# Two-layer graph network on one core: left scores through memory, a reordered front, a third adjacency pair held on chip, degrees from layer 1, and the last pair by tile

## The chip, the core and the metric

The kernel runs on one core of a Trainium2 chip. The engines of the core work side by side, each through its own list of instructions in order: TensorE (PE, with its weight loads PEld), VectorE (DVE), ScalarE (ACT), GpSimd (POOL), and SyncE (SP), which here only issues transfers. They wait for each other on semaphores. The metric is the device time of one execution, in microseconds (us); smaller is better.

## What is computed

```
deg = max(sum(adj != 0), 1)
h   = relu(layernorm(x))                                   # x: 3327 x 256, adj: 3327 x 3327, zeros and ones
x   = x + L0(h, adj)
h   = relu(layernorm(x))
x   = x + relu((dinv * (adj + I) * dinv @ h + h) @ W + b)  # dinv = rsqrt(deg)

L0(x, adj):
  attn_a = sigmoid([adj @ x, x] @ Wa.T + ba);  attn_b the same with Wb, bb
  h = x @ W_sa;  s_left = h @ a_sa[:256];  s_right = h @ a_sa[256:]
  e = where(adj != 0, exp(-leaky_relu(s_left[:, None] + s_right[None, :], 0.01)), 0)
  x_a = (e / (sum(e, axis=1) + 1e-5)) @ h
  x_b = adj @ (x @ W_gcnb) + b_gcnb
  return sigmoid(attn_a * x_a + attn_b * x_b)
```

The "layer 1" of the title is the first of the two layers (the one with scores), "layer 2" below the last one. In the code names with a trailing 1 (`dense1`, `HI1`, `pooled`) belong to the last layer.

## The kernel before

The 3327 rows stand in 26 tiles of 128, taken as 13 pairs (`PAIRS`); `LAST` is 12. Wide products are made of 16-bit halves, `HI` and `LO` of a value, so that each product of two matrices is two or three matmuls per tile.

**The front** (first loop on PE, `for s in range(PAIRS)`) prepares `h` of pair after pair. Per pair `s`: ACT normalises (`norm`, line 448), PE turns the tile (`turn`, L610), ACT copies it twice (`turned`, L455 and L456), DVE makes the low half (`turned_second`, L899), PE projects to six score columns (`project`, L638), DVE takes them (`take_scores`, L907), PE multiplies with both weights (`dense`, 12 matmuls of 512 columns, L656 to L658), ACT and DVE take the two halves `HI` and `LO` (`first_halves` L469, `second_halves` L914). DVE also takes the statistics of two later pairs (`row_stats`, L843, L847), POOL their inverse deviations (`inv_stds`, L327, L329). The left score of every row has to stand in every partition: POOL spreads it on a diagonal (`diag`, L337), PE multiplies that with ones (`widen`, L644), and ACT copies it (`left`, L473) to `slw`, which shares its memory with `LO1`. `keep_busy` (L622) gives PE matmuls on ones whose result nobody reads: 42 ahead of the first `dense`, and 4 behind each of the first two. From step 4 on PE does the first products of layer 1 in between (`neighbours` with m = 0 on the adjacency, `unit` on the exponentials).

**Layer 1** goes over the pairs `m`: ACT makes the exponentials of pair m (`leaky` L485, `expo` L494), DVE masks and splits them (L939, L945), PE does 13 `unit`s (12 matmuls each, L703 to L705) and 13 `neighbours` (8 matmuls each, L682 and L683) of the pair behind. The adjacency of a pair is loaded by POOL's queue to `stage`, transposed by DVE (`turn_adj`, L931) to one of two buffers `adjT`, and stored by SP's queue to memory (`adjT_store`).

**Layer 2** (`pooled(k, u)`, L754 and L755, 8 matmuls) takes the pairs in the order `ORDER` = 11, 12, 0, 1, ..., 10. The first two are still in the two `adjT` buffers; each later one is loaded back in two chunks (u below 6, and the rest) by SP as soon as the buffer's last chunk is done (L292). Three accumulators take turns. A column of ones behind `HI1` gives the degrees; DVE's `output` (L1100 to L1117) takes the maximum with 1, the inverse, adds the self term from POOL and the residual, and ACT's queue stores 256 KB per pair.

What sets the order everywhere is the order in which each engine's list is written; an engine that waits holds all that stands behind.

Of the kernel before, what the change touches and what calls it, by code (L numbers as in the profile page):

```python
# [19 lines left out]
def gnn_kernel(nc, x, adj, W_sa, a_sa, W_g, b_g, Wa, ba, Wb, bb, W1, b1, out):  # L20
# [29 lines left out]
    with ExitStack() as ctx:  # L50
# [8 lines left out]

        adjT_store = nc.dram_tensor("adjT_store", [PAIRS, P, PAIRS * 256], U32, kind="Internal").ap()  # L60
# [4 lines left out]
        HI1 = sb("HI1", [P, TILES, D + 2], F16)  # L65
# [25 lines left out]
        diag = sb("diag", [P, 2, P])  # L91
# [11 lines left out]
        degm = sb("degm", [P, 2])  # L103
        drp = sb("drp", [P, 2])
        drw = sb("drw", [P, 2])
# [24 lines left out]
        slw = LO1[:].rearrange("p (m e) d -> p m (e d)", e=2).bitcast(F32)  # L130

# [42 lines left out]
        diag_ok = sem("diag_ok")  # L174
        wide = sem("wide")
        sl_ok = sem("sl_ok")
# [42 lines left out]
        one1_ok = sem("one1_ok")  # L219
        lo1_ok = sem("lo1_ok")  # L220
        adj_ld = [[sem(f"adj_ld{c}_{b}") for b in range(2)] for c in range(NC)]
# [6 lines left out]
        deg_c = sem("deg_c")  # L228
        drp_ok = sem("drp_ok")
        drw_ok = sem("drw_ok")  # L230
        pt_c = sem("pt_c")
# [28 lines left out]
        def out_count(k, b):  # L260
            return 16 * sum(3 if ORDER[j] == LAST else 1 for j in range(k + 1) if j % 2 == b)
# [4 lines left out]
        def _(sp):  # L266
            for k, w in enumerate((W_sa, W_g)):
                sp.dma_start(wsg[k], w.rearrange("(h p) o -> p h o", p=P)).then_inc(wsg_in, 16)
            load_x(sp, 0, (2, 3))
# [7 lines left out]
            sp.dma_start(w1, W1.rearrange("(h p) o -> p h o", p=P)).then_inc(w1_in, 16)  # L277
            sp.dma_start(bgrep[:], bass.AP(b_g.tensor, 0, [[0, P], [1, D]])).then_inc(rep_in, 16)
            sp.dma_start(b1rep[:], bass.AP(b1.tensor, 0, [[0, P], [1, D]])).then_inc(rep_in, 16)

            for m in range(LAST - 1):
                sp.wait_ge(tr_ok, NC * (m + 1))
                sp.dma_start(adjT_store[m], adjT[m % 2][:].rearrange("p u e i v -> p (u e i v)").bitcast(U32)
                             ).then_inc(stored[m % 2], 16)
            for b in range(2):
                sp.wait_ge(stored[b], 16 * len(range(b, LAST - 1, 2)))

            for k in range(2, PAIRS):
                for c, (u0, u1) in enumerate(CHUNKS):
                    sp.wait_ge(part_done[c], k - 1)  # L290
                    dst = adjT[(k + 1) % 2][:, u0:u1].rearrange("p u e i v -> p (u e i v)").bitcast(U32)
                    sp.dma_start(dst, adjT_store[ORDER[k], :, 256 * u0:256 * u1]).then_inc(adj_ld[c][k % 2], 16)  # L292
# [853 lines left out]
```

## Time and profile before

| | us |
|---|---|
| median of 3 runs | 653.65 |
| lowest, highest | 652.34, 656.84 |
| profiled execution, device time | 648.95 |
| its span, first to last instruction | 647.1 |
| PE busy in it | 617.8 (95%) |
| DVE, ACT, POOL busy | 438.2, 365.3, 271.5 |

The profile shows one execution. PE's matmuls overlap, so that a busy PE may still start matmuls at a slow pace; how many it starts in a stretch and the clock it was granted say more. Idle time ahead of an instruction is listed with what ended it. Idle time of an engine that nobody waits for costs nothing.

### The profile page before, as it was taken

The numbers are of one execution on the slowest core, as the hardware profiler recorded it, in microseconds if no ns is written. First come the engines' busy times: TensorE is split into PE (matmuls) and PEld (weight loads), VectorE is DVE, ScalarE is ACT, GpSimd is POOL, SyncE is SP. The second block draws the span as 40 slices with busy tenths as digits, with TensorE's granted clock in tenths as the row PEclk, the third lists the DMA queues.
The fourth block names the chain that finished last, engine by engine and source line by source line (L and its number), as shares of the span: only waits on it lengthen the run. The fifth ranks groups of instructions, "written<-read, shape, count | busy, mean of one in ns | idle before, by whom it ended". The sixth has DMA issues, their size and how long they took to land.

```text
span 647.1 us, 13487 instructions
## 1 busy us (share of the span) xinstructions
PE 617.8 (95%) x5333; PEld 528.0 (82%) x5333; DVE 438.2 (68%) x869; ACT 365.3 (56%) x877; POOL 271.5 (42%) x378
## 2 busy tenths in 40 slices
PE   6777999999999999999999999999999799999994
PEld 3445677888888888888888888888888688888883
DVE  4577665799999898989898988988752323122131
ACT  2566676779888787878787777879632000000000
POOL 3547463355435162435353366313134253425331
PEclk9798999999999999999999999999999999999998
DMA  8904572397364554656563644000010365555521
GB/s 201 194 4 131 81 170 44 50 195 180 51 164 89 124 142 74 156 80 160 73 164 53 164 50 58 2 1 2 1 51 2 115 244 172 171 161 178 183 76 32
DMA packets 38549, 68.62 MB, mean 106 GB/s; under 512 B 3159, under 2 KB 30809, under 8 KB 37079
## 3 DMA queue, kind: packets, MB, share of 16 engines
q0 software_dynamic: 28544, 22.15, 23.6%
q1 hardware_dynamic: 7906, 41.68, 19.8%
q10 hardware_dynamic: 2037, 3.94, 2.3%
q8 instruction: 42, 0.69, 0.4%
q14 instruction: 20, 0.16, 0.1%
HBM read 67.74 MB, written 22.15 MB: 139 GB/s over the span
## 4 chain that ended last, share of the span: by engine, by line
PE 87%; POOL 4%; DVE 3%; issue 2%; DMA 1%; ACT 1%; ACTq 0%; POOLq 0%; DVEq 0%
PE accE L703 11%; PE accE L705 11%; PE accA L682 11%; PE accE L704 11%; PE accA L683 11%; PE accA L755 8%; PE accA L754 8%; PE accE L754 4%; PE accE L755 4%; POOL diag L337 1%; PE tp L610 1%; POOL stage L317 1%; PE pw L726 1%; PE pw L727 1%; PE pw L728 1%
## 5 line engine op out<-in xcount | busy, mean ns | idle before, releaser
L703 PE MATMUL accE<-HI,Z 128*128 128x257 f16 x676 | 184.3, 273 | 0.0
L705 PE MATMUL accE<-HI,E 128*128 128x257 f16 x676 | 184.1, 272 | 0.0
L704 PE MATMUL accE<-LO,Z 128*128 128x256 f16 x676 | 183.9, 272 | 0.0
L485 ACT ACTIVATE Z<-LO,sr 128x256 f32<-128x256 f32 x338 | 151.3, 497 | 40.0 <-PE accE L705 40.0
L682 PE MATMUL accA<-HI,adjT 128*128 128x258 f16 x676 | 154.1, 273 | 0.0
L683 PE MATMUL accA<-LO,adjT 128*128 128x258 f16 x676 | 154.0, 273 | 0.0
L494 ACT ACTIVATE Z<-Z,sr 128x256 f32<-128x256 f32 x338 | 150.2, 497 | 0.1
L945 DVE TENSOR_TENSOR E<-Z 128x512 bf16<-128x512 f32 x169 | 140.7, 832 | 5.8
L939 DVE TENSOR_TENSOR Z<-adjT,Z 128x512 f32<-128x512 bf16 x169 | 120.3, 712 | 18.8 <-ACT Z L494 18.6
L755 PE MATMUL accA<-LO,adjT 128*128 128x256 f16 x468 | 103.5, 273 | 0.0
L754 PE MATMUL accA<-HI,adjT 128*128 128x257 f16 x468 | 103.5, 273 | 0.0
L317 POOL DMA_DIRECT2D stage<-in_adj_dram x96 | 59.6, 655 | 98.8 <-DVE adjT L931 94.5
L683 PEld LDWEIGHTS accA<-LO,adjT 128*128 128x128 bf16 x676 | 66.0, 98 | 8.9
L682 PEld LDWEIGHTS accA<-HI,adjT 128*128 128x128 bf16 x676 | 66.0, 98 | 8.8
L704 PEld LDWEIGHTS accE<-LO,Z 128*128 128x128 bf16 x676 | 65.8, 97 | 8.4
L705 PEld LDWEIGHTS accE<-HI,E 128*128 128x128 bf16 x676 | 65.7, 97 | 8.5
L703 PEld LDWEIGHTS accE<-HI,Z 128*128 128x128 bf16 x676 | 65.8, 97 | 8.4
L423 POOL TENSOR_TENSOR late<-HI,LO 128x512 f32<-128x512 f16 x13 | 20.0, 1538 | 79.8 <-DVE wx L1112 77.8
L931 DVE STREAM_TRANSPOSE adjT<-stage 128x768 uint32<-128x768 uint32 (+1 forms) x52 | 51.0, 1017 | 0.0
L754 PE MATMUL accE<-HI,adjT 128*128 128x257 f16 x208 | 47.2, 278 | 3.9 <-DMA adjT<-adjT_store 3.9
L754 PEld LDWEIGHTS accA<-HI,adjT 128*128 128x128 bf16 x468 | 45.8, 98 | 5.7
L755 PEld LDWEIGHTS accA<-LO,adjT 128*128 128x128 bf16 x468 | 45.8, 98 | 5.3
(116 smaller groups left out, 761.6 us busy)
## 6 DMA issues: line engine op xcount, KB each, us to landing
adjT_store<-adjT SPq DMA_DIRECT2D x11, 1664.0 KB, 6.7
adjT<-adjT_store SPq DMA_DIRECT2D x11, 896.0 KB, 4.7
stage<-in_adj_dram POOLq DMA_DIRECT2D x48, 192.0 KB, 5.0
adjT<-adjT_store SPq DMA_DIRECT2D x11, 768.0 KB, 6.3
stage<-in_adj_dram POOLq DMA_DIRECT2D x36, 224.0 KB, 8.1
out_dram<-late ACTq DMA_DIRECT2D x12, 256.0 KB
stage<-in_adj_dram POOLq DMA_DIRECT2D x12, 223.5 KB, 9.7
xs<-in_x_dram SPq DMA_DIRECT2D x5, 256.0 KB, 6.0
```

What stands on the lines that cost most here:

```text
L317: pool.dma_start(stage[32 * b:32 * b + 32, :, :, w0:w1_], src).then_inc(adj_in[c], 16)
L485: ins = act.activation(Z[:, n % RING, v], slw[:, m], ACT.Relu, bias=sr99[:, t:t + 1], scale=1.0 - SLOPE)
L494: ins = act.activation(Z[:, n % RING, v], Z[:, n % RING, v], ACT.Exp, bias=sr01[:, t:t + 1], scale=-1.0)
L682: pe.matmul(dst, w, HI[:, t, G0:HIW], start=(t == 0), stop=False)
L683: ins = pe.matmul(dst, w, LO[:, t, D:LOW], start=False, stop=(t == TILES - 1))
L703: pe.matmul(dst[:, 0:D + 1], zhi, HI[:, t, 0:D + 1], start=(t == 0), stop=False)
L704: pe.matmul(dst[:, 0:D], zhi, LO[:, t, 0:D], start=False, stop=False)
L705: ins = pe.matmul(dst[:, 0:D + 1], zlo, HI[:, t, 0:D + 1], start=False, stop=(t == TILES - 1))
L754: pe.matmul(dst[:, 0:D + 1], w, HI1[:, t, 0:D + 1], start=(t == 0), stop=False)
L755: ins = pe.matmul(dst[:, 0:D], w, LO1[:, t, :], start=False, stop=(t == TILES - 1))
L939: dve.tensor_tensor(Z[:, n % RING], rows, Z[:, n % RING], ALU.mult).then_inc(mask_ok, 1)
L945: dve.tensor_tensor(E2[:, n % RING], Z[:, n % RING], hi, ALU.subtract).then_inc(e2_ok, 1)
```

## The change

1. **Left scores through memory.** `diag`, `widen` and `left` are gone. SP stores the column of left scores of a pair (128 x 2 numbers of 4 bytes) to `sl_store` in memory, waits until it is there, and loads it back to all partitions (128 KB) as `slw`. `project` now waits for `srw_ok` where it waited for `left`.
2. **Front reordered.** SP loads half of the first x group ahead of `W_sa`; ACT's queue loads the other half, then `W_g`. DVE takes the first statistics before the weights' scales. The first `dense` stands ahead of `turn(1)` and `project(0)`; ACT's `norm(1)` stands behind `first_weights`. `W1` and the two bias rows are loaded behind the first left scores.
3. **No idle products.** `keep_busy` is gone.
4. **Third pair kept.** In layer 2 the memory of `stage`, free by then, is a third adjacency buffer. The pair k = 2 is loaded to it during layer 1, and each pair k from 3 on goes where k - 3 was. PE's order at the change of layers takes `pooled(2, u)` where it took the last `pooled(0, u)` and `pooled(1, u)`.
5. **Degrees from layer 1.** The ones column comes in with `neighbours`: its first matmul has 260 columns instead of 258, the second still 258, written two columns further on. ACT copies the degree column per pair; DVE forms the inverse once for all tiles. `pooled` has 256 columns instead of 257 in its first matmul, and `output` is three instructions on DVE. POOL scales the self term per tile.
6. **Last pair by tile.** The last pair of layer 2 does all its e = 0 matmuls, then all e = 1, with output and store by tile.

```diff
@@ sync
-            for k, w in enumerate((W_sa, W_g)):
-                sp.dma_start(wsg[k], w.rearrange("(h p) o -> p h o", p=P)).then_inc(wsg_in, 16)
-            load_x(sp, 0, (2, 3))
+            load_x(sp, 0, (0, 1))
+            sp.dma_start(wsg[0], W_sa.rearrange("(h p) o -> p h o", p=P)).then_inc(wsg_in, 16)
...
+            def spread_left(i):
+                sp.wait_ge(srw_ok, i + 1)
+                sp.dma_start(bass.AP(sl_store.tensor, 2 * P * i, [[1, P], [P, 2]]), srw[:, 2 * i:2 * i + 2, 3],
+                             allow_slow_non_contiguous=True).then_inc(sl_out, 16)
+                sp.wait_ge(sl_out, 16 * (i + 1))
+                if i >= 1:
+                    sp.wait_ge(sl_in, 16 * i)
+                sp.dma_start(slw[:, i], bass.AP(sl_store.tensor, 2 * P * i, [[0, P], [1, 2 * P]])).then_inc(sl_in, 16)
...
+            for i in range(PAIRS):
+                spread_left(i)
+                if i == 0:
+                    sp.dma_start(w1, W1.rearrange("(h p) o -> p h o", p=P)).then_inc(w1_in, 16)
...
+                if i == 6:
+                    keep_adj(0)
+            for m in range(1, LAST - 1):
+                keep_adj(m)
...
+            sp.wait_ge(tr_ok, NC * PAIRS)
             for k in range(2, PAIRS):
                 for c, (u0, u1) in enumerate(CHUNKS):
-                    sp.wait_ge(part_done[c], k - 1)
-                    dst = adjT[(k + 1) % 2][:, u0:u1].rearrange("p u e i v -> p (u e i v)").bitcast(U32)
+                    if k >= 3:
+                        sp.wait_ge(part_done[c], k - 2)
+                    dst = adj1[k % 3][:, u0:u1].rearrange("p u e i v -> p (u e i v)").bitcast(U32)
...
@@ gpsimd, score_parts
-                if i >= 1:
-                    pool.wait_ge(wide, i)
-                for e in range(2):
-                    ins = pool.tensor_scalar(diag[:, e], ident[:], srw[:, 2 * i + e, 3:4], None, ALU.mult)
-                ins.then_inc(diag_ok, 1)
...
@@ scalar
-            load_x(act, 0, (0, 1))
+            load_x(act, 0, (2, 3))
+            act.dma_start(wsg[1], W_g.rearrange("(h p) o -> p h o", p=P)).then_inc(wsg_in, 16)
...
             def leaky(m, u):
                 n = m * PAIRS + u
-                if n == 0:
-                    act.wait_ge(sl_ok, 1)
+                if u == 0:
+                    act.wait_ge(sl_in, 16 * (m + 1))
...
+                act.activation(degs[:, 2 * m:2 * m + 2], accA[m % 2][:].rearrange("p (e n) -> p e n", e=2)[:, :, 0],
+                               ACT.Copy)
...
@@ tensor, neighbours
-                        dst = bank(accA[m % 2], e)[:, 0:D + 2]
-                        pe.matmul(dst, w, HI[:, t, G0:HIW], start=(t == 0), stop=False)
-                        ins = pe.matmul(dst, w, LO[:, t, D:LOW], start=False, stop=(t == TILES - 1))
+                        dst = bank(accA[m % 2], e)
+                        pe.matmul(dst[:, 0:D + 4], w, HI[:, t, ONE:HIW], start=(t == 0), stop=False)
+                        ins = pe.matmul(dst[:, 2:D + 4], w, LO[:, t, D:LOW], start=False, stop=(t == TILES - 1))
...
@@ tensor, change of layers
-            pooled(0, LAST - 2)
-            pooled(1, LAST - 2)
+            for u in range(2):
+                pooled(2, u)
             turn1(LAST)
-            pooled(0, LAST - 1)
-            pooled(1, LAST - 1)
+            for u in range(2, 5):
+                pooled(2, u)
             dense1(LAST)
-            for u in range(6):
+            for u in range(5, 8):
                 pooled(2, u)
-            pooled(0, LAST)
-            pooled(1, LAST)
-            for u in range(6, PAIRS):
+            for k in range(2):
+                for u in range(10, PAIRS):
+                    pooled(k, u)
+            for u in range(8, PAIRS):
                 pooled(2, u)
-            for k in range(3, PAIRS):
+            for k in range(3, LAST):
                 for u in range(PAIRS):
                     pooled(k, u)
+            for e in range(2):
+                pooled_tile(LAST, e)
...
@@ vector
+            def pooled_out(k, e):
+                t = 2 * ORDER[k] + e
+                dve.scalar_tensor_tensor(out=[wx, wm][k % 2][:, e], in0=bank([accA[1], accA[0], accE][k % 3], e)[:, 0:D],
+                                         scalar=drw[:, t:t + 1], in1=hpw[:, e], op0=ALU.mult,
+                                         op1=ALU.add).then_inc(y_ok, 1)
```

On PE, in the front, these rows stand before from the last matmul of the first `dense` to the first of the second (`accA<-wh` is `dense`, `accA<-ones` is `keep_busy`, `pw<-diag` is `widen`, `tp` is `turn`, `pw<-w` is `project`):

```order
L658 MATMUL accA<-wh,hTl 128x512
L622 MATMUL accA<-ones 128x256 x4
L644 MATMUL pw<-diag,ones 128x256
L610 MATMUL tp<-ident,hf 128x128 x4
L638 MATMUL pw<-w,hT 128x6 x4
L656 MATMUL accA<-wh,hTh 128x512
```

And the same place in the changed kernel:

```order
L667 MATMUL accA<-wh,hTl 128x512
L629 MATMUL tp<-ident,hf 128x128 x4
L652 MATMUL pw<-w,hT 128x6 x4
L629 MATMUL tp<-ident,hf 128x128 x4
L652 MATMUL pw<-w,hT 128x6 x4
L665 MATMUL accA<-wh,hTh 128x512
```

The filling and the `widen` are gone, and `turn(1)` and `project(0)`, which stood ahead of the first `dense`, stand behind it.

On DVE, at the start of the program, before (`wabs`, `ub`, `wmax`, `winv` are the scales of the weights, `bst`, `mv` the statistics of x, `nmr` is what ACT's `norm` waits for, `wl` what `dense` waits for):

```order
L1014 COPY w<-pw 128x4
L1015 COPY w<-pw 128x4
L869 TENSOR_REDUCE wabs<-late 128x1 x2
L869 TENSOR_REDUCE wabs<-w 128x1
L873 TENSOR_SCALAR ub<-ident,wabs 128x128 x3
L843 BN_STATS bst<-xs 128x6 x2
L847 BN_AGGR mv<-bst 128x2 x2
L878 TENSOR_REDUCE wmax<-accE 128x3
L882 TENSOR_SCALAR wmax<-wmax 128x3
L884 RECIPROCAL winv<-wmax 128x3
L853 SCALAR_TENSOR_TENSOR nmr<-mv,rstd 128x2
```

and in the changed kernel:

```order
L862 BN_STATS bst<-xs 128x6 x2
L866 BN_AGGR mv<-bst 128x2 x2
L1035 COPY w<-pw 128x4
L1036 COPY w<-pw 128x4
L888 TENSOR_REDUCE wabs<-late 128x1 x2
L872 SCALAR_TENSOR_TENSOR nmr<-mv,rstd 128x2
L888 TENSOR_REDUCE wabs<-w 128x1
L894 TENSOR_SCALAR ub<-ident,wabs 128x128 x3
```

The first statistics and `nmr` moved ahead of most of the scales; `score_weights` moved behind the weights' low halves.

On SP, at the change of layers, before (with what each waits for):

```order
L283 DMA adjT_store<-adjT 128x3328 [waits tr_ok] x11
L292 DMA adjT<-adjT_store 128x1536 [waits part_done0,stored1,stored0]
L292 DMA adjT<-adjT_store 128x1792 [waits part_done1]
L292 DMA adjT<-adjT_store 128x1536 [waits part_done0]
L292 DMA adjT<-adjT_store 128x1792 [waits part_done1]
```

and in the changed kernel:

```order
L293 DMA adjT_store<-adjT 128x3328 [waits tr_ok] x10
L315 DMA stage<-adjT_store 128x1536 [waits tr_ok,stored1,stored0]
L315 DMA stage<-adjT_store 128x1792
L315 DMA adjT<-adjT_store 128x1536 [waits part_done0]
L315 DMA adjT<-adjT_store 128x1792 [waits part_done1]
```

The first load of layer 2 waits for no matmul of layer 2 any more, and goes to `stage`.

## Rows read from the trace of the kernel before

**Rows 1.** The page, busy time and the granted clock in 40 slices.

```profile
PE 617.8 (95%) x5333; PEld 528.0 (82%) x5333; DVE 438.2 (68%) x869; ACT 365.3 (56%) x877; POOL 271.5 (42%) x378
PEclk9798999999999999999999999999999999999998
```

**Rows 2.** Waits of PE: who waited for whom, total us, times, longest.

```profile
PE pw L644 <- POOL diag L337: 7.1, 6, 2.3
PE accE L754 <- DMA adjT<-adjT_store: 3.9, 1, 3.9
```

**Rows 3.** Stretches: length, busy us (instructions) per engine, clock, DMA share, GB/s.

```profile
19.00:20.00 1.00, 0.71 (x2) 0.29 (x3) 0.96 (x5) 0.00 (x0) 0.00 (x0) 0.50 1.10 217
20.00:30.00 10.00, 8.70 (x38) 4.30 (x37) 5.27 (x22) 4.62 (x9) 6.82 (x13) 0.78 1.25 213
120.00:160.00 40.00, 40.00 (x367) 35.43 (x365) 37.11 (x65) 35.01 (x88) 20.27 (x26) 1.00 0.77 162
510.00:520.00 10.00, 6.14 (x44) 4.70 (x43) 5.62 (x16) 0.00 (x0) 4.84 (x4) 0.83 0.72 279
```

**Rows 4.** Timeline, start of the program: start us, us, instruction, idle before.

```profile
6.64 0.27 PE L627 MATMUL pw<-ident,wrows 8*128 8x8 f32 x1 [1.40 <-DMA wrows<-in_L_gnn_Wb_dram]
12.05 1.09 ACT L448 ACTIVATE hf<-xs,nmr,rstd 128x256 f32<-128x256 f32 x2 [7.50 <-DVE nmr L853]
17.12 1.42 DVE L893 SCALAR_TENSOR_TENSOR wl<-late,winv,wh 128x512 f16<-128x512 f32 x2 [2.80 <-ACT wh L462]
19.29 0.59 PE L656 MATMUL accA<-wh,hTh 128*128 128x512 f16 x1 [0.88 <-DVE hTl L899]
```

**Rows 5.** Timeline, step 2 to step 3 of the front.

```profile
37.35 1.20 POOL L337 TENSOR_SCALAR diag<-ident,srw 128x128 f32<-128x128 f32 x2
38.60 0.70 PE L644 MATMUL pw<-diag,ones 128*128 128x256 f32 x2 [1.59 <-POOL diag L337]
40.75 0.38 PE L656 MATMUL accA<-wh,hTh 128*128 128x512 f16 x1
43.12 0.38 PE L658 MATMUL accA<-wh,hTl 128*128 128x512 f16 x1
```

**Rows 6.** Timeline, first matmul of the `dense` of steps 7 and 12.

```profile
70.56 0.38 PE L656 MATMUL accA<-wh,hTh 128*128 128x512 f16 x1
103.31 0.38 PE L656 MATMUL accA<-wh,hTh 128*128 128x512 f16 x1
```

**Rows 7.** Groups, 19 to 60 us (POOL 0 to 60): count, busy us, mean ns, idle.

```profile
L843 DVE BATCH_NORM_STATS2 bst<-xs 128x6 f32<-128x256 f32 x22 | 8.0, 408 | 0.0
L914 DVE TENSOR_TENSOR LO<-accA,HI 128x512 f16<-128x512 f32 x11 | 7.1, 685 | 6.9 <-ACT HI L469 6.9
L899 DVE TENSOR_TENSOR hTl<-hT,hTh 128x512 f16<-128x512 f32 x7 | 4.8, 685 | 0.0
L931 DVE STREAM_TRANSPOSE adjT<-stage 128x896 uint32<-128x896 uint32 x2 | 2.1, 1082 | 0.0
L329 POOL TENSOR_TENSOR rstd<-ve,halfs 128x4 f32<-128x4 f32 x3 | 3.1, 1038 | 0.2
```

**Rows 8.** Groups of PE over the whole span.

```profile
L644 PE MATMUL pw<-diag,ones 128*128 128x256 f32 x26 | 9.0, 429 | 7.1 <-POOL diag L337 7.1
L682 PE MATMUL accA<-HI,adjT 128*128 128x258 f16 x676 | 154.1, 273 | 0.0
```

**Rows 9.** Transfers: name, queue, count, KB each, median us from issue to landing.

```profile
bias<-in_L_gnn_ba_dram SPq DMA_DIRECT2D x1, 0.5 KB, 5.1
late<-in_L_gnn_W_dram SPq DMA_DIRECT2D x1, 256.0 KB, 16.6
adjT<-adjT_store SPq DMA_DIRECT2D x11, 896.0 KB, 4.7
```

**Rows 10.** Timeline, end of the program.

```profile
638.08 0.22 DVE L1100 TENSOR_SCALAR degm<-accA 128x1 f32<-128x1 f32 x2 [8.60 <-PE accA L755]
639.27 0.88 DVE L1112 SCALAR_TENSOR_TENSOR wx<-wm,drw,late 128x256 f32<-128x256 f32 x2
640.19 0.69 DVE L1117 SCALAR_TENSOR_TENSOR late<-wx,xs 128x512 f32<-128x512 f32 x1
```

More of the change, by code:

```diff
@@ L130, in gnn_kernel @@
         slw = LO1[:].rearrange("p (m e) d -> p m (e d)", e=2).bitcast(F32)
+        adj1 = [adjT[1][:], adjT[0][:],
+                stage[:].rearrange("p e b q -> p (e b q)").rearrange("p (u e i v) -> p u e i v", u=PAIRS, e=2, v=2)]
         accE = ps("accE", 2)
@@ L218, in gnn_kernel @@
         hi1_ok = sem("hi1_ok")
-        one1_ok = sem("one1_ok")
         lo1_ok = sem("lo1_ok")
-        adj_ld = [[sem(f"adj_ld{c}_{b}") for b in range(2)] for c in range(NC)]
+        adj_ld = [[sem(f"adj_ld{c}_{b}") for b in range(3)] for c in range(NC)]
         part_done = [sem(f"part_done{c}") for c in range(NC)]
@@ L260, in out_count @@
         def out_count(k, b):
-            return 16 * sum(3 if ORDER[j] == LAST else 1 for j in range(k + 1) if j % 2 == b)
+            return 16 * sum({LAST: 3, LAST - 2: 2}.get(ORDER[j], 1) for j in range(k + 1) if j % 2 == b)
         block = ctx.enter_context(nc.Block())
@@ L276, in _, with keep_adj @@
             load_x(sp, 3)
[L277 to L281, printed above, removed]
+            def spread_left(i):
[6 more added lines that the diff above has]
+                sp.dma_start(slw[:, i], bass.AP(sl_store.tensor, 2 * P * i, [[0, P], [1, 2 * P]])).then_inc(sl_in, 16)
+            def keep_adj(m):
                 sp.wait_ge(tr_ok, NC * (m + 1))
@@ L414, in _ @@
             inv_std1(LAST)
-            one_column(LAST)
             def self_term(k):
@@ L538, in _ @@
             first_weights(1)
+            norm(1)
             for s in range(PAIRS + 5):
@@ L587, in store_out @@
                 m = ORDER[k]
+                if k == LAST:
+                    for e in range(2):
+                        act.wait_ge(o_ok, k + 1 + e)
+                        dst = bass.AP(out.tensor, (m * 64 + e) * D, [[QN * D, 4], [2 * D, QUAD], [1, D]])
+                        act.dma_start(dst, osb[k % 2][:, e]).then_inc(o_out[k % 2], 16)
+                    return
                 act.wait_ge(o_ok, k + 1)
@@ L618, in turn @@
                 transposes(tp, hf[:, i % 2]).then_inc(hT_ps, 1)
-            def keep_busy(n):
-                for _ in range(n):
-                    pe.matmul(accA[0][:, 0:2 * P], ones[:].bitcast(BF16)[:, 0:P], ones[:].bitcast(BF16), start=True,
-                              stop=True)
             def turn_weights():
@@ L640, in project @@
                 ins.then_inc(proj, 1)
-            def widen(i):
-                pe.wait_ge(diag_ok, i + 1)
-                pe.matmul(pw[:, 256:512], ones[:], diag[:].rearrange("p e n -> p (e n)"), start=True,
-                          stop=True).then_inc(wide, 1)
             def dense(i):
```

167 lines of the change are left out of this document (92 added, 75 removed).

## The prediction

> **What bounds the kernel now.** I read the page first: PE is busy for 95% of the span, the clock row is at 9 or below in a few slices at the front, and 9 elsewhere [rows 1]. A busy PE is not yet a PE that does work at pace, so I went to the stretches. In layer 1 it starts 367 matmuls in 40 us, 0.109 us each, without a gap, at the 2.4 GHz level [rows 3]; there nothing but fewer or shorter matmuls helps. Two stretches are not like that. Between 20 and 30 us PE starts 38 matmuls at a mean clock of 0.78, and between 510 and 520 us it starts 44 where the pace gives 93 [rows 3]. The list of waits then names what PE waited for: 7.1 us for POOL's `diag` in the front, and once 3.9 us for the adjacency that comes back from memory at the change of layers [rows 2]. Last comes the end of the program, where PE has stopped and a chain on DVE and a store remain [rows 10]. So the kernel is PE's list plus a front that several engines share, one hole at the change of layers, and a tail. The change touches all three, and layer 1 hardly.
>
> **The start.** Before, the first `dense` begins at 19.29 [rows 4], behind `norm(0)` at 12.05 on ACT, `norm(1)`, two turns and `project(0)`. Its 12 matmuls of 512 columns run at the 1.2 GHz level (the clock of 0.50 in the first row of [rows 3]), 0.43 us each, 5.1 us. The changed order: x is first in both queues, so I put the first statistics at 5.3 to 6.3, the deviations at 7.4, and `nmr` behind the two large scales at 8.9 (these wait for `wrows`, which PE had at 6.64 [rows 4]; one more transfer ahead of it makes that about 7.0). `norm(0)` 8.9 to 10.1, but `turn(0)` waits in PE's list for the spread of the scales, to 12.0. Two copies to 13.1, two `first_weights` to 14.4, two low halves on DVE (1.42 for both [rows 4]) to 15.2. The first `dense` starts at 15.2, 4.1 us earlier. The 42 idle products ahead of it are worth nothing to it before: it ran at the low level in spite of them [rows 3]. Behind it now stand `turn(1)` and `project(0)`, 1.7 us, `turn(2)`, which waits for `norm(2)` until 23.7, and `project(1)`: the second `dense` begins at 25.2.
>
> **The steps 1 to 6.** From one `dense` to the next PE cannot go faster than dense 2.6 us (12 x 0.216, which is 43.12 - 40.75 over 11 [rows 5]), the high half of one tile on ACT 0.6, and its low half on DVE 0.69 [rows 7]: about 4.1 us. Before, PE's list held `widen` in that path: in step 2 `diag` began on POOL at 37.35, `widen` at 38.60, and the next `dense` at 40.75 [rows 5]. With `diag`, `widen` and `left` gone, what is late next is DVE: two statistics (2 x 2 x 0.41 and the aggregates, 2.0 together), hTl 0.69, LO 2 x 0.69 per step [rows 7], and in steps 1 and 2 it also waits for POOL's deviations, 1.04 [rows 7] behind the statistics. Writing each instruction behind the later of its engine's last one and its releaser, I get `dense` of step 1 to 6 at 25.2, 30.3, 35.7, 39.9, 47.1 and 54.8. Steps 4 and 5 are long since DVE has `turn_adj` (2.1 for its two halves of the second chunk [rows 7]), the scale of `W1` and the first mask there. `dense` of step 7 follows at 60.9, where it was at 70.56 [rows 6].
>
> **The steps 7 to 12.** PE is the bound. From 70.56 to 103.31 are five steps, 6.55 each [rows 6]. A `widen` is two matmuls, 0.43 us [rows 8], and some 0.1 per step was wait for `diag`; 6.03 stay. Step 12 is at 91.0, 12.3 us earlier, and its own `widen` adds 0.4: **12.7 us** if the clock holds at 2.4 GHz.
>
> **The clock.** Fewer matmuls in the gaps let it fall more easily. Before, it was down from before 19 to beyond 24 us although filled, and up afterwards [rows 3]. I charge one of the sparse places (behind the first `dense`, or step 4) two thirds of a `dense` at half pace, 2.6 x 0.65 = **1.7 us**. Front: 12.7 - 1.7 = **11.0 us**. Bounds: 0 to five denses at half pace, 13 us.
>
> **Through memory.** SP's queue carries a store of 256 numbers of 4 bytes and a load of 128 KB per pair. No row has this store; the nearest is the bias, 128 numbers of 4 bytes to 128 partitions, 5.1 us in a busy queue [rows 9]; the worst in that queue is W1's 16.6 [rows 9]. The first left scores are there at 22.4; with the x loads still ahead in the queue I take 6 for the store and 4 for the load, there by 33 (bounds 4 and 33 us for both, from those rows). ACT needs them for the first `leaky` at 39.6: hidden, with 7 us in hand. Behind the waiting SP stand the load of W1, which DVE needs at 42.5 in step 3, and the store of the first adjacency, which DVE needs only after the front. The other 12 pairs are needed one per 30 us in layer 1. Cost 0; each microsecond beyond 39.6 (or for W1 beyond 42.5) would be one on DVE's and PE's path. The Trainium skill (DMA: Bandwidth & Descriptors, "Rules for kernel authors") says that a last dimension which isn't contiguous becomes one descriptor per element, and advises to rearrange it; that rule speaks against this store. By it the cost is in the queue, off the path above, and the sum stays; the rows before can't show its size.
>
> **Layer 1.** 676 matmuls get two more columns [rows 8], 2 / 2.4 ns each, +0.56 us; 676 in layer 2 lose one, -0.28. Together **+0.3 us**. ACT gets one small copy per pair, at most 0.4 us in 30, in a stretch where it is busy 35 of 40 us and PE never waits [rows 3]: 0. Uncovered it would be 13 x 0.4 = 5 us.
>
> **The change of layers.** 93 - 44 = 49 matmuls are missing between 510 and 520 us [rows 3], x 0.109 = **5.4 us**: the wait of 3.9 and the matmuls at half clock behind it. `stage` is free after the last transposition, long before; its load waits for no product of layer 2. Next in line is pair k = 3: its second chunk can be loaded when `pooled(0, 12)` is done, and until it is needed PE has 3 + 5 + 6 groups of 8 matmuls, 12 us, against 4.7 for 896 KB [rows 9]. POOL's self term (about 5 us) and DVE's `output(0)` end inside that time too. All 5.4 are gained.
>
> **The tail.** Before, 638.08 to 640.88 is DVE's chain on 256 rows [rows 10], then the store until 647.1. Now the last tile needs one of the two L1112, 0.44, and half of L1117, about 0.4, with a gap: 0.9 instead of 2.8, **1.9 us**. The store of half the size I count as equal.
>
> **Sum.** 11.0 + 5.4 + 1.9 - 0.3 = 18.0 us. The profiled execution goes from 648.95 to 631. It was 4.7 us under the median of the runs; I take the difference from the median: 653.65 - 18 = **635.5 us**.
>
> **The rivals.**
> *The clock stays low through the front.* For it: without filling the gaps behind each `dense` hold only turns and projections, and around 53 us, before, a light step was already enough to show in the page's row [rows 1]. Against it: between step 2 and 3, before, `dense` found only a `widen`, a turn and a projection ahead of it and still ran at 0.216 per matmul [rows 5]. Price: steps 1 to 5 each some 1.8 us longer, 9 us instead of 1.7; gain 10.7, 643 us. The Trainium skill (TensorE: Matmul & The Clock Gate, "Why this matters for your kernels") asks for TensorE to be kept busy and warns of gaps between bursts; by it this rival is the likelier, and the time is the 643 just worked out. The row of step 2 to 3 says otherwise here, but it had `widen` in it. Chance 0.17.
> *The left scores or W1 come late.* ACT or DVE stands in step 3. With both transfers at the far bound, 33 us from 22.4, that is 55 instead of 39.6, but leaky only holds `unit`: PE loses perhaps 6 us. 641.5 us. Chance 0.09.
> *A new wait takes the place of the load's.* The last turn and `dense1` of the change now find fewer groups ahead, or the self term is late for `output(0)`; the 5.4 stay. 641 us. Chance 0.06.
> *The shifted output slows `neighbours`.* Two matmuls per pair of tiles now write overlapping but unequal columns, the second from the third column on. No row has such a write. It would touch 2 x 676 matmuls; from 18.0 / 1352 = 13 ns more for each the whole gain is gone, and at 25 ns the kernel takes 635.5 + 34 = 669 us, slower. Against it: the forms of 258 and 257 columns with different starts all run at 0.109 us each among each other [rows 3]. Chance 0.03.
>
> **How the numbers follow.** Forecast 0.65; the clock 0.17; late transfers 0.09; new wait 0.06; slower 0.03. The forecast's own range is 631.5 to 639 (the clock term 0 to 4, the start plus or minus 1.5, and the spread of the runs). The range that leaves out no more than 2 in 10 reaches to the clock's 643: 631.5 to 643.5. A measurement of this kernel tells about 1% from no change, 6.5 us: all cases but the last give more in their middle; from the far ends of the clock and the late transfers I leave 0.05 within 1%. Faster 0.92, same 0.05, slower 0.03.
>
> **What would show it.** The first `dense` at about 15, the one of step 7 at about 61, of step 12 at about 91; no `diag` among PE's waits, and in its place, in steps 3 to 5, waits for DVE. No wait for `adjT_store`, and 92 or 93 matmuls in every 10 us around the change of layers. Some 7 us from DVE's first instruction behind the last matmul to the end of the span, instead of 9.0. The load of `sl_store` landed before ACT's first L485. I am wrong if PE waits for ACT or DVE behind a late transfer, if more than one more `dense` runs at 0.43 per matmul, or if layer 1 starts fewer than 365 matmuls in 40 us.

## Result and the profile after

| | before | after |
|---|---|---|
| median (4 runs each, same chip) | 655.25 us | 690.25 us |
| lowest, highest | 652.34, 656.96 | 688.05, 691.98 |
| profiled execution, its span | 648.95, 647.1 | 688.05, 686.2 |
| PE busy in it | 617.8 | 604.7 |

The ratio is 1.0537, interval 1.048 to 1.0594: 5.4% slower, where 2.8% faster was forecast. PE has less to do, 13 us less, and stands still. The page, beside [rows 1]; the two rows are 40 slices of the span (busy share and granted clock in tenths):

```profile
PE 604.7 (88%) x5257; PEld 518.7 (76%) x5257; DVE 424.9 (62%) x809; ACT 361.8 (53%) x877; POOL 259.8 (38%) x352
PE   2889899160099999999999999999999999999997
PEclk9899999685589999999999999999999999999999
PE 73%; DMA 23%; SPq 1%; DVE 1%; issue 0%; ACTq 0%; ACT 0%; DVEq 0%
```

PE stands still twice, from about 120 to 135 us and from 149 to 190 us, and DMA has 23% of the chain that ended last. The list of waits (engine, line, what it waited for: us in total, times, longest), beside [rows 2]:

```profile
DVE adjT L952 <- DMA adjT_store<-adjT: 58.8, 2, 42.9
PE accE L712 <- DVE E L966: 44.2, 5, 40.9
PE accE L712 <- DVE wm L1004: 15.4, 1, 15.4
```

The 7.1 us for `diag` and the 3.9 us for `adjT_store` on PE [rows 2] are gone. In their place DVE waits twice, 58.8 us, for a store: the adjacency of an old pair has to be in memory before DVE may turn a new one into its buffer. PE's two long waits are for DVE behind that. SP's timeline says why the store is late (start us, duration, engine, line, operation; "..." marks more pairs of the same kind):

```profile
21.25 0.40 SPq L284 DMA_DIRECT2D sl_store<-srw  x1
33.74 0.35 SPq L289 DMA_DIRECT2D LO<-sl_store  x1
...
94.80 0.67 SPq L284 DMA_DIRECT2D sl_store<-srw  x1
107.09 0.32 SPq L289 DMA_DIRECT2D LO<-sl_store  x1
107.46 2.06 SPq L293 DMA_DIRECT2D adjT_store<-adjT  x1
...
178.07 0.32 SPq L289 DMA_DIRECT2D LO<-sl_store  x1
178.43 21.32 SPq L293 DMA_DIRECT2D adjT_store<-adjT  x3
```

Each pair's left scores are stored (L284) and waited for; then the load (L289) is issued and SP goes on to the next pair's store, beside which the load lands. Seven pairs take 107.46 - 21.25 = 86 us, 12.3 each. The adjacency of pair 0 is issued behind the seventh, at 107.46, that of pair 1 behind the thirteenth, at 178.43. Before, the first was issued at 56.97. The end of the second hole on the chain that ended last (start, us, what):

```profile
167.71 10.34 DMA sl_store<-srw
...
178.43 8.38 DMA adjT_store<-adjT
...
187.84 0.94 DVE adjT L952
...
190.13 0.40 PE accE L712
```

Three stretches (us, then busy time and starts of PE, weight loads, DVE, ACT, POOL; clock; DMA share; GB/s), two in the second hole and one in layer 1 behind it:

```profile
150.00:160.00 10.00, 0.00 (x0) 0.00 (x0) 0.00 (x0) 0.00 (x0) 0.00 (x0) 0.60 0.20 29
170.00:180.00 10.00, 0.00 (x0) 0.00 (x0) 0.00 (x0) 0.00 (x0) 0.00 (x0) 0.50 0.28 13
200.00:300.00 100.00, 100.00 (x912) 88.67 (x910) 93.16 (x163) 82.03 (x205) 42.52 (x51) 1.00 0.61 130
```

In the hole no engine computes anything, and the transfers move 13 to 29 GB/s: the chip waits for the completion of one transfer of 1 KB at a time. Afterwards layer 1 runs at its old pace, 0.110 us per matmul as in [rows 3].

The difference of the spans, split at places that both traces have: `dense` of step 12 starts at 92.91 instead of 103.31 [rows 6], -10.4. The last transposition in layer 1 starts at 551.39 instead of 502.00, +49.4, so the stretch from step 12 to it gained +59.8. From there to DVE's first instruction behind the last matmul it is 130.2 instead of 136.1, -5.9. From that to the end 4.6 instead of 9.0 [rows 10], -4.4. Together +39.1, which is 686.2 - 647.1. The front's 10.4 us are no gain in the end: the hole ends when SP's chain does, and whoever comes to it earlier waits longer.

### The profile page after: what moved, and what is told of

The parts are those of the page before. It is cut to its first block, busy times and chain, and to the rows that moved or that the text cites. A ratio compares the mean times of both kernels' runs of the same rounds, so it can differ in the third digit from the quotient of the medians.

```text
span 686.2 us, 13267 instructions
## 1 busy us (share of the span) xinstructions
PE 604.7 (88%) x5257; PEld 518.7 (76%) x5257; DVE 424.9 (62%) x809; ACT 361.8 (53%) x877; POOL 259.8 (38%) x352
## 2 busy tenths in 40 slices
DMA packets 44090, 70.33 MB, mean 102 GB/s; under 512 B 6908, under 2 KB 36478, under 8 KB 42620
## 4 chain that ended last, share of the span: by engine, by line
PE 73%; DMA 23%; SPq 1%; DVE 1%; issue 0%; ACTq 0%; ACT 0%; DVEq 0%
DMA sl_store<-srw 22%; PE accE L712 10%; PE accE L714 10%; PE accE L713 9%; PE accA L691 9%; PE accA L692 9%; PE accA L762 7%; PE accA L761 7%; PE accE L762 3%; PE accE L761 3%; DMA adjT_store<-adjT 1%; PE tp L629 1%; PE accA L778 1%; PE pw L736 1%; PE pw L734 1%; PE pw L735 1%
## 5 line engine op out<-in xcount | busy, mean ns | idle before, releaser
L691 PE MATMUL accA<-HI,adjT 128*128 128x260 f16 x676 | 154.2, 274 | 1.3 <-DVE adjT L952 1.3
L960 DVE TENSOR_TENSOR Z<-adjT,Z 128x512 f32<-128x512 bf16 x169 | 120.3, 712 | 18.9 <-ACT Z L507 18.7
L762 PE MATMUL accA<-LO,adjT 128*128 128x256 f16 x416 | 91.6, 273 | 0.0
L761 PE MATMUL accA<-HI,adjT 128*128 128x256 f16 x416 | 91.6, 273 | 0.0
L952 DVE STREAM_TRANSPOSE adjT<-stage 128x768 uint32<-128x768 uint32 (+1 forms) x52 | 51.0, 1018 | 64.1 <-DMA adjT_store<-adjT 58.8
L691 PEld LDWEIGHTS accA<-HI,adjT 128*128 128x128 bf16 x676 | 65.8, 97 | 10.8 <-DVE adjT L952 1.4
L692 PEld LDWEIGHTS accA<-LO,adjT 128*128 128x128 bf16 x676 | 65.9, 97 | 8.8
L762 PE MATMUL accE<-LO,stage 128*128 128x256 f16 x208 | 45.8, 273 | 0.0
L761 PE MATMUL accE<-HI,stage 128*128 128x256 f16 x208 | 45.8, 273 | 0.0
L761 PEld LDWEIGHTS accA<-HI,adjT 128*128 128x128 bf16 x416 | 40.6, 98 | 4.8
L762 PEld LDWEIGHTS accA<-LO,adjT 128*128 128x128 bf16 x416 | 40.7, 98 | 4.7
```

The source lines that it names most:

```text
L691: pe.matmul(dst[:, 0:D + 4], w, HI[:, t, ONE:HIW], start=(t == 0), stop=False)
L692: ins = pe.matmul(dst[:, 2:D + 4], w, LO[:, t, D:LOW], start=False, stop=(t == TILES - 1))
L761: pe.matmul(dst, w, HI1[:, t, :], start=(t == 0), stop=False)
L762: ins = pe.matmul(dst, w, LO1[:, t, :], start=False, stop=(t == TILES - 1))
L960: dve.tensor_tensor(Z[:, n % RING], rows, Z[:, n % RING], ALU.mult).then_inc(mask_ok, 1)
```

## The experiments

The theory after the result (A): SP's list is too slow for what stands behind it, and only the two late adjacency stores cost. Its rival (B): the many small pieces themselves load the DMA engines, whatever the order. And the gains that the prediction counted (front, change of layers, tail) are to be found behind the loss, or not. Kernels with a ratio were run four times; the others once.

**Only SP's order.** Two lines; adjacency stores stand between the left scores:

```diff
-                if i == 6:
-                    keep_adj(0)
-            for m in range(1, LAST - 1):
+                if i in {2: 0, 4: 1, 7: 2, 9: 3}:
+                    keep_adj({2: 0, 4: 1, 7: 2, 9: 3}[i])
+            for m in range(4, LAST - 1):
```

> The changed kernel with SP's list reordered and nothing else: the stores of the adjacency of pairs 0, 1, 2 and 3 stand behind the left scores of pairs 2, 4, 7 and 9 instead of behind those of pair 6 (pair 0) and 12 (the rest). In the changed kernel the profile shows a store of left scores to take 9 to 13 us, thirteen in series on SP, so the adjacency store of pair 0 is issued at 107 us and that of pair 1 at 178 us, and DVE waits 15.9 and 42.9 us for them. Theory A (SP's order: the adjacency stores stand behind a chain of slow round trips): both waits go, 59 us less than the changed kernel, span about 628, ratio to the kernel before about 0.970. Theory B (3328 small descriptors load the 16 DMA engines and slow every transfer): they are all still there, so most of the loss stays, span over 670. Theory C (a wait for the left scores themselves takes over, since they are spread one every 12 us): leaky of a later pair waits; span between 635 and 670.

Measured: 636.78 us, ratio 0.9749 (0.9687 to 0.981), span 633.4. 53 us of the changed kernel's 690 come from the place of four stores. The span is 5 us above the expected 628. No wait for `adjT_store` is left. Its own waits:

```profile
DVE adjT L952 <- DMA stage<-in_adj_dram: 11.8, 3, 8.0
PE accE L712 <- DVE E L966: 7.0, 3, 5.8
```

So something of (B) remains: DVE now waits for POOL's loads of the adjacency. The page's transfers issued from 52 to 90 us (number, KB each, median us to landing), in this kernel and in the one before:

```profile
stage<-in_adj_dram POOLq DMA_DIRECT2D x6, 224.0 KB, 17.5
```

```profile
stage<-in_adj_dram POOLq DMA_DIRECT2D x3, 224.0 KB, 7.4
```

The same load takes more than twice as long beside the stores of small pieces.

**The left scores on the chip again**, all else as changed: `diag`, `widen` and `left` are back, `spread_left` is gone, SP's order is as before.

```diff
+            def widen(i):
+                pe.wait_ge(diag_ok, i + 1)
+                pe.matmul(pw[:, 256:512], ones[:], diag[:].rearrange("p e n -> p (e n)"), start=True,
+                          stop=True).then_inc(wide, 1)
```

> The changed kernel with part 1 undone: left scores are spread on the chip again by diag, widen and left, as before; all other parts stay, and the adjacency stores are issued as soon as they are ready. Theory A: no wait for an adjacency store; against e1 it pays widen on PE (13 x 0.43 = 5.6 us) and some waits of PE for POOL's diag (7 us before, of which I expect 3 to stay), so a span of about 635 to 638, ratio 0.98. Theory B: about the same, since the small descriptors are gone too. If other parts of the change (reordered front, third buffer, degrees) were what slowed it, this one is slower than the kernel before.

Measured: 644.28 us, ratio 0.9865 (0.9801 to 0.9929), span 640.0. PE waits for `diag` as before:

```profile
PE pw L656 <- POOL diag L347: 6.8, 4, 2.4
```

The span is 2 us above the expected 635 to 638. Its `dense` of step 12 starts at 106.06, no earlier than before (103.31 [rows 6]), although the first `dense` starts at 15.34. That alone doesn't show that the gain of the front is all part 1's, since this kernel has no idle products either and ran the `dense` of steps 1, 3 and 5 at 1.2 GHz; the kernel with the memory path alone, below, shows it. Of the span the change of layers and the tail save 10.2 us, and what lies ahead of them loses 3.1.

**Fewer pieces in the store.** POOL copies the two scores of a pair side by side, so that a store is 128 pieces of 8 bytes instead of 256 of 4; ACT reads them with a step of two. SP's order is that of the change, late stores and all.

```diff
+                pool.tensor_copy(slc[:, tiles], srw[:, tiles, 3]).then_inc(slc_ok, 1)
-                sp.dma_start(bass.AP(sl_store.tensor, 2 * P * i, [[1, P], [P, 2]]), srw[:, 2 * i:2 * i + 2, 3],
-                              allow_slow_non_contiguous=True).then_inc(sl_out, 16)
+                sp.dma_start(bass.AP(sl_store.tensor, 2 * P * i, [[2, P], [1, 2]]),
+                              slc[:, 2 * i:2 * i + 2]).then_inc(sl_out, 16)
```

> The changed kernel in its own order on SP, but POOL first copies the two score columns side by side, the store writes 128 pieces of 8 bytes instead of 256 of 4, and ACT reads the loaded row with a step of two. If a store's 9 to 13 us go by pieces: half, 5 to 6 us; seven of them keep pace with the front, the store of pair 0 is issued near 70 us, of pair 1 near 110 us, and no wait is left: span about 630. If they are a fixed round trip: 9 to 13 us again and the span stays near 686.

Measured, one run: 626.63 us, span 624.8, better than both kernels. SP's timeline of it:

```profile
30.57 0.43 SPq L286 DMA_DIRECT2D sl_store<-slc  x1
35.13 0.33 SPq L291 DMA_DIRECT2D LO<-sl_store  x1
...
69.73 0.43 SPq L295 DMA_DIRECT2D adjT_store<-adjT  x1
...
112.82 83.29 SPq L295 DMA_DIRECT2D adjT_store<-adjT  x5
```

The store lands in 3.8 to 7.4 us (10.5 once, right behind an adjacency store), and the two adjacency stores are issued at 69.73 and 112.82 instead of 107.46 and 178.43, early enough without touching the order. And POOL's loads are fast again:

```profile
stage<-in_adj_dram POOLq DMA_DIRECT2D x6, 224.0 KB, 6.9
```

**The same kernel, timed.**

> The kernel of e3 once more, timed: all of the change, the store of the left scores in 128 pieces of 8 bytes, SP's order as in the change. e3's single run gave 626.6 us, span 624.8. I expect 627 to 630, ratio about 0.963. If e3 was a lucky run, it is near e1 (635).

Measured: 625.91 us, ratio 0.9564 (0.9504 to 0.9624), span 622.9: 4.4% faster than before, the best of the study. Against the kernel with only SP's order changed it is 10.5 us of span. The two differ in the pieces and in where the stores stand; in neither does anything wait for `adjT_store`. The 11.8 us of DVE's waits for `stage` are gone. Not all of the 10.5 is (B)'s share: 1.4 us of it are there at step 7 already (`dense` at 59.28 against 60.72), where the second `dense` ran at 2.4 GHz in this execution and at 1.2 GHz in the other. Most of the rest, 7.4 us, lies between steps 7 and 12, where DVE waits for the loads. The runs don't divide it between the pieces and the earlier adjacency stores that are under way at the same time.

**Is it the number of pieces or the stride of the source?** The copy stays, but the store goes to the old places in memory, so it is 256 pieces of 4 bytes from a contiguous source; ACT reads the scores as in the change.

```diff
-                sp.dma_start(bass.AP(sl_store.tensor, 2 * P * i, [[2, P], [1, 2]]),
+                sp.dma_start(bass.AP(sl_store.tensor, 2 * P * i, [[1, P], [P, 2]]),
```

> Between the changed kernel and e5: POOL copies the two score columns side by side, but the store still writes 256 pieces of 4 bytes, tile by tile, as in the change; ACT reads as in the change. If the number of pieces sets the store's time: 9 to 13 us again, the adjacency loads land in some 15 us, and the span is near 686. If the step of the source column did: 4 to 7 us and a span near 625.

Measured, one run: 684.27 us, span 682.5. The first store and one at the end of the front, from its chain that ended last:

```profile
22.70 10.83 DMA sl_store<-slc
...
104.97 13.35 DMA sl_store<-slc
```

and `stage` takes 12.7 us, where the kernel with 128 pieces, otherwise the same, had 6.9. The number of pieces (and with it their size) sets both; how they lie on the chip doesn't matter. With SP's order as it is, though, this contention costs little by itself: from step 7 to step 12 it is 30.2 us here and 29.7 there.

**The memory path alone**, on the kernel before: only part 1, in its 4-byte form and with SP's order of the change.

```diff
-                widen(s)
+            for i in range(PAIRS):
+                spread_left(i)
...
+                if i == 6:
+                    keep_adj(0)
```

> The kernel before with part 1 alone: left scores through memory in pieces of 4 bytes, SP's list with the adjacency store of pair 0 behind the left scores of pair 6 and the rest behind the last; front order, idle products, two buffers and all else as before. Theory A: SP's chain of 13 round trips of 12 us is the same, so is the wait at pairs 2 and 3; about 8 us are gained in the front and none of it is seen, since the chain sets the time: the store of pair 1 issued near 180 us, span near 700, that is 50 us or more above the kernel before. If the loss needed another part of the change (the reordered front or the third buffer's wait on SP), this one is no slower than before.

Measured, one run: 689.82 us, span 688.0.

```profile
DVE adjT L928 <- DMA adjT_store<-adjT: 48.3, 2, 40.0
169.39 20.99 SPq L287 DMA_DIRECT2D adjT_store<-adjT  x3
```

Part 1 alone makes the whole loss, 41 us of span, less than the expected 50. It also makes nearly the whole gain of the front. Its `dense` of steps 7 and 12:

```profile
60.76 0.38 PE L655 MATMUL accA<-wh,hTh 128*128 128x512 f16 x1
...
94.06 0.38 PE L655 MATMUL accA<-wh,hTh 128*128 128x512 f16 x1
```

They were at 70.56 and 103.31 before [rows 6] and are at 60.65 and 92.91 in the changed kernel, although this one's first `dense` starts at 19.33 as before: of the 4 us by which the reordered front brings the start forward little is left at step 7. The levels differ, though: the second `dense` ran at 2.4 GHz here and at 1.2 in the changed kernel. Against the best kernel, which had it at 2.4 too and step 7 at 59.28, 1.5 us are left. That the other parts, worth some 10 us behind the hole, don't show as such between this span and the 686.2 of the changed kernel is the chain's own spread: here pair 1's store was issued at 169.39, there at 178.43, and with it the hole ended 9 us sooner.

**Only one more store moved**: pair 0 and pair 1 behind the seventh and eighth left scores, the rest behind the last.

```diff
-                if i == 6:
-                    keep_adj(0)
+                if i in {6: 0, 7: 1}:
+                    keep_adj({6: 0, 7: 1}[i])
```

> The changed kernel with one line of SP's list moved: the adjacency store of pair 1 stands behind the left scores of pair 7, that of pair 0 stays behind pair 6. If the order on SP sets the loss in amount too: pair 0's store is late as in the changed kernel (PE waits about 15 us), pair 1's is issued near 122 us instead of 178 and DVE needs it some 45 us after pair 0's, so the 41 us wait goes: span 686 - 41 to 43 = about 644. If the loss is contention, it stays near 686.

Measured, one run: 658.23 us, span 656.4, where about 644 was expected: a miss. It saved 30 us of span, where 41 to 43 were expected; then pair 2 was in the place of pair 1:

```profile
DVE adjT L952 <- DMA adjT_store<-adjT: 35.2, 2, 23.4
...
177.97 0.91 SPq L293 DMA_DIRECT2D adjT_store<-adjT  x2
```

The expectation repeated the prediction's mistake: it looked at the transfer that was late and not at the next one in the list, which still stood behind all 13 left scores. The kernel with four stores moved has no such wait.

**The idle products back**, on the kernel with SP's order mended: 42 ahead of the first `dense`, 4 behind each of the first two.

```diff
+            keep_busy(16)
             turn_weights()
+            keep_busy(10)
...
+                if s < 2:
+                    keep_busy(4)
```

> e1 with the 50 idle products back at the same places (16, 10, 10, 6 ahead of the first dense, 4 behind each of the first two). In the changed kernel both first denses ran at 0.43 us per matmul, the second from 25.0 to 29.6 us. Clock theory: with the filling the second dense runs at 0.216, the third starts 1 to 2.5 us earlier, and the kernel is up to 2 us faster than e1. Rival: the filling only lies in PE's way (behind the first dense 4 x 0.21 = 0.9 us) and it is the same as e1 or 1 us slower.

Measured: 636.27 us, ratio 0.9734 (0.9675 to 0.9792), against 0.9749 without them, with intervals that overlap almost wholly: worth nothing. The stretch of the second `dense`, first in the changed kernel, then in this one; the clock is the third number from the end:

```profile
25.00:30.00 5.00, 5.00 (x17) 2.11 (x18) 1.93 (x9) 0.94 (x3) 2.59 (x7) 0.59 1.66 112
```

```profile
25.00:30.00 5.00, 5.00 (x16) 2.42 (x16) 2.85 (x12) 1.69 (x4) 2.59 (x7) 0.50 1.52 61
```

The second `dense` is slow in both. The fill gave the first `dense` the 2.4 GHz level (0.39 us for its first matmul instead of 0.61), but that `dense` then began at 17.39 instead of the 15.73 of the same kernel without fill, 1.7 us later. The prediction's sentence that the fill is worth nothing holds; its reason (the first `dense` is slow in spite of it) is true of the kernel before, not of this one.

**The change of layers undone**, on the best kernel: two buffers instead of three and PE's old order there.

```diff
-        adj1 = [adjT[1][:], adjT[0][:],
-                stage[:].rearrange("p e b q -> p (e b q)").rearrange("p (u e i v) -> p u e i v", u=PAIRS, e=2, v=2)]
+        adj1 = [adjT[1][:], adjT[0][:]]
```

> e5 with the third adjacency buffer undone: two buffers, the loads and PE's order at the change of layers as before. In the kernel before, 49 matmuls of 0.109 us were missing there, 5.4 us; in the changed kernel the stretch from the last turn (L629) to the first output of the last pair is 5.9 us shorter than before, of which 0.3 are the narrower matmuls. Third-buffer theory: 5 to 6 us slower than e5. Rival (the order of PE at the change filled the hole, or the hole only shows because layer 1 ends as it does): within 2 us of e5.

Measured: 633.07 us, ratio 0.9674 (0.9614 to 0.9734), span 632.0. From the last transposition to the end it takes 141.9 us, and 134.8 in the best kernel: part 4 is worth 7.1 us, against 5 to 6 expected. (The spans differ by 9.1; the other 2.0 are there at step 12 already, 91.03 against 89.02.) The wait of [rows 2] and the slow stretch of [rows 3] are back:

```profile
PE accE L762 <- DMA adjT<-adjT_store: 4.2, 1, 4.2
495.00:505.00 10.00, 5.83 (x53) 4.95 (x52) 2.27 (x7) 0.00 (x0) 7.13 (x7) 0.93 0.43 152
505.00:515.00 10.00, 10.00 (x70) 7.93 (x69) 2.76 (x6) 0.00 (x0) 5.65 (x6) 0.73 0.63 240
```

Against 92 per 10 us, 39 + 22 = 61 matmuls are missing, 6.7 us. The prediction's 49 were all that the kernel before lacked (48 per 5 us on both sides of its slow stretch), so its 5.4 was right for that trace; here the slow part is longer.

**The last pair whole**, on the best kernel: `pooled` and `output` as for the others, one store of 256 KB.

```diff
-            for k in range(LAST):
+            for k in range(PAIRS):
...
-            for e in range(2):
-                output_tile(LAST, e)
```

> e5 with the last pair as a whole again: one output and one store of 256 KB. From DVE's first instruction behind the last matmul to the end of the span it was 9.0 us before and 4.6 us in the changed kernel; the sum in the prediction had 1.9 us for it, from DVE alone. If the shorter store of half the size is worth the other 2.5 us: DVE's chain with the new three-instruction output is about 1.8, the store about 6.2, so this kernel is some 3.4 us slower than e5 in the trace. Rival (the store's time is that of the completion and doesn't go by size): 0.9 us slower.

Measured: 631.06 us, ratio 0.9623 (0.9552 to 0.9693), span 629.7. DVE's instructions behind the last matmul, here and in the best kernel (the changed kernel's two stand at 681.56 and 682.08, with the same durations):

```profile
621.83 0.88 DVE L1126 SCALAR_TENSOR_TENSOR wx<-accA,drw,late 128x256 f32<-128x256 f32 x2 [9.75 <-PE accA L760]
622.75 0.69 DVE L1141 SCALAR_TENSOR_TENSOR late<-wx,xs 128x512 f32<-128x512 f32 x1
```

```profile
618.23 0.48 DVE L1134 SCALAR_TENSOR_TENSOR wx<-accA,drw,late 128x256 f32<-128x256 f32 x1 [4.44 <-PE accA L782]
```

From there to the end 629.7 - 621.83 = 7.87 us against 622.9 - 618.23 = 4.67: 3.2 us. DVE has 0.7 of it (1.6 against 0.9); the other 2.5 are a shorter time from DVE's last instruction to the end. Of that the prediction said "The store of half the size I count as equal". The spans differ by 6.8; the other 3.6 are there at step 12 already (92.63 against 89.02), with the second `dense` and most of that of step 3 at 1.2 GHz.

## Why the prediction was wrong

**The step that failed is the one called "Through memory"**: the size of the store, and more so what it was laid against in the sentence on what stands "Behind the waiting SP". The store was taken at 6 us, from the bias load of 5.1 [rows 9]; it measured 9.3 to 13.2. And its cost was put at 0 because ACT needs one pair's scores late. But a queue whose entries wait for each other is a chain, and what stands behind the chain has its own due time. A link of it is the store alone, since the load (5.0 us in the median) lands beside the next pair's store: the adjacency of pair 0 stands behind 7 stores, that of pair 1 behind 13. When are they needed? DVE's timeline of the kernel before has it:

```profile
115.61 1.83 DVE L931 STREAM_TRANSPOSE adjT<-stage 128x768 uint32<-128x768 uint32 x2
...
138.45 1.83 DVE L931 STREAM_TRANSPOSE adjT<-stage 128x768 uint32<-128x768 uint32 x2
```

These turn pairs 2 and 3 over pairs 0 and 1. With a front 12 us shorter they would start at 104 and 126. The page of the kernel before has the time from an adjacency store's issue to its landing (KB, median us):

```profile
adjT_store<-adjT SPq DMA_DIRECT2D x11, 1664.0 KB, 6.7
```

So pair 0's has to be issued by 97 and pair 1's by 119. From the prediction's 22.4 on that leaves at most 10.7 us for each of 7 stores, and at most 7.5 us for each of 13 (estimates, from these rows). At the prediction's own 6 us the list would have been in time, and in the best kernel it is: 115.42 - 23.37 = 92.1 us for 13, 7.1 each. At the measured 12.3 the chain is 13 x 4.8 = 62 us too long, and DVE waited 58.8. The stated bounds, 4 and 33 us, had both cases inside; yet the sum charged 0 for all of them up to ACT's 39.6, and one for one beyond, where from 7.5 on each microsecond costs 13. The sentence spoke of "the store of the first adjacency", needed "only after the front", and passed over the second. The remark "one per 30 us in layer 1" was made for the scores and hid that the chain doesn't know who needs what. The kernel with moved stores (same store, other order), the one with fewer pieces (same order, faster store) and the one with part 1 alone show this mechanism; by the run with moved stores it is 53 of the 55 us between forecast (635.5) and result (690.25). The rest nearly cancels: the contention below against gains larger than forecast at the front, the change of layers and the tail; without either fault the best kernel stands at 625.91, 10 us under the forecast.

**Contention was put at nothing.** The prediction weighed the rule of the Trainium skill (DMA: Bandwidth & Descriptors, "Rules for kernel authors") that a last dimension which isn't contiguous becomes one descriptor per element, and put its cost "in the queue, off the path above, and the sum stays". The runs agree with the rule: the page of the changed kernel counts 44090 packets and that of the kernel with 128 pieces 42425, 1665 fewer, where 13 x 128 is 1664. In time, 256 pieces take 9 to 13 us, whether the source is contiguous or not, and 128 mostly 4 to 8. They contradict the conclusion: the queue was the path, and such a store also holds up POOL's loads, 12.7 to 18.0 us against 6.9 to 8.3. In the changed kernel DVE waits 5.3 us for them; with the adjacency stores moved forward 11.8 us, and the steps 7 to 12 take 37.2 us instead of the best kernel's 29.7.

**The front was right in its mechanism**, and its number in part by luck. From the trace after:

```profile
15.28 0.61 PE L665 MATMUL accA<-wh,hTh 128*128 128x512 f16 x1 [3.30 <-DVE wl L914]
25.00 0.59 PE L665 MATMUL accA<-wh,hTh 128*128 128x512 f16 x1
60.65 0.38 PE L665 MATMUL accA<-wh,hTh 128*128 128x512 f16 x1
92.91 0.38 PE L665 MATMUL accA<-wh,hTh 128*128 128x512 f16 x1
```

Predicted were 15.2, 25.2, 60.9 and 91.0, the last two ahead of 1.7 for the clock. In the best kernel the second, that of step 7 and that of step 12 are:

```profile
24.55 0.38 PE L669 MATMUL accA<-wh,hTh 128*128 128x512 f16 x1
...
59.28 0.38 PE L669 MATMUL accA<-wh,hTh 128*128 128x512 f16 x1
...
89.02 0.38 PE L669 MATMUL accA<-wh,hTh 128*128 128x512 f16 x1
```

With step 12's own `widen` (0.4) the forecast was 12.7 without and 11.0 with the clock term; after shows 10.8, the best kernel 14.7. That 10.8 meets 11.0 is in part luck: step 7 came on time with a slow `dense` already in it, and from there to step 12 it took 32.3 us instead of the forecast 30.1, while DVE waited 5.3 us for `stage`. The clock term had the right size for this execution: one more `dense` ran slowly, the second. Whether it does isn't fixed by the kernel: the best kernel's other profiled execution had it at 1.2 GHz, and its step 7 at 61.21, 1.9 us later.

```profile
25.23 0.59 PE L669 MATMUL accA<-wh,hTh 128*128 128x512 f16 x1
```

That part 1 (no `diag`, no `widen`, no `left`) freed the front is shown by the kernel with that part alone: 9.2 us earlier at step 12.

**The change of layers** was forecast at 5.4 and the tail at 1.9. After shows 5.9 - 0.3 of columns and 4.4; the runs that undo them show 7.1 and 3.2 (there part 5's shorter `output` stays). Mechanisms right; DVE's chain shrank from 2.8 to 0.9 us as forecast, and the tail's term was too small by the shorter store (2.5 us by the run that undoes it).

**Layer 1 and the shifted output.** The two groups of the products with the adjacency, all 1352 of them, with mean ns beside [rows 8]:

```profile
L691 PE MATMUL accA<-HI,adjT 128*128 128x260 f16 x676 | 154.2, 274 | 1.3 <-DVE adjT L952 1.3
L692 PE MATMUL accA<-LO,adjT 128*128 128x258 f16 x676 | 154.1, 273 | 0.0
```

At 912 matmuls in 100 us the pace is unchanged; the rival that a shifted output slows them is refuted, and it was the only one on the slower side. The rival "late transfers" had the right transfers, but looked only at scores and `W1`: ACT had no listed wait for the scores and DVE none for `W1`. The right case was not among them, so that the chance of slower, 0.03, was far too low.

**What stays open.** The changed kernel with four stores moved and fewer pieces at once was not run; whether it would gain over the best kernel isn't known, but in that one DVE waits for no store and no load of the adjacency. It has little in hand: the store of pair 1 is issued at 115.42, and DVE turns pair 3 over it at 124.40.

## What to carry over

When a wait is put into an engine's list of transfers, write out that list with its times: each entry's issue is the sum of all round trips ahead of it, and each later entry is laid against its own due time in the trace of before, the second and third as well as the first. A round trip through memory is cheap once and dear thirteen times in series; either put what is urgent between, or have fewer pieces per store. A transfer of many tiny pieces is counted by its pieces, and charged to the loads of other queues too.

## What was not expected of the hardware

- A store of 1 KB took mostly 9 to 13 us as 256 pieces of 4 bytes (9.3 to 13.2 in the changed kernel, 9.6 to 13.4 with a contiguous source), and mostly 4 to 8 us as 128 pieces of 8 bytes. Right behind an adjacency store of 1664 KB it took up to 18.9 and 12.5 us.
- Beside the former, loads of 224 KB from another queue took 12.7 to 18.0 us (medians, 52 to 90 us); beside the latter 6.9 to 8.3; before, 7.4.
- The end of the program, last DVE instruction to end of span, is some 2.5 us shorter with a last store of 128 KB than with one of 256 KB.
- 42 idle products brought the first `dense` to the 2.4 GHz level and delayed it by 1.7 us in one kernel; in the kernel before and in the one with part 1 alone the same 42 left it at 1.2 GHz. The second `dense` was at either level with them (2.4 GHz with part 1 alone, 1.2 in the kernel that has them back) and without (of two executions of the best kernel one had it at 2.4 and one at 1.2). What decides that stays open.
